# A two-layer conditioned residual kernel: transposed output with its column factor applied at eviction, three of eight weight products summed in PSUM, and unrolled loops

## The reference

```python
ae = layernorm(cond, g, b); h = gelu(ae @ w1 + b1); xw = h @ w2 + b2     # w2 is 512 x 8192
x_a, x_b = split(xw)                       # each [8, 512, 8]
layer = base_layer + x_a @ x_b^T           # per batch, 512 x 512
x = x + (x + x @ layer)                    # = x @ (2 I + layer)
ys = cond / sqrt(512)
d  = rsqrt((ys*ys) @ (W*W) + 1e-8)         # [8, 512], W = L1 weight
x = x + ((x * ys) @ W) * d                 # = x @ (I + diag(ys) W diag(d))
```

## Time and profile before

| | us |
|---|---|
| runs | 321.42, 321.53, 321.64 |
| span of the profiled execution | 319.6 |
| runs' median less that span | 1.93 |
| PE busy (share of the span) | 307.4 (96%) |
| DVE busy | 157.8 (49%) |
| ACT busy | 135.8 (42%) |
| POOL busy | 43.2 (14%) |

### The profile page before, as it was taken

One profiled execution on the slowest core, in us unless ns is written; L12 is line 12 of the kernel. 1 busy time (PEld: TensorE's weight loads), 2 busy tenths in 40 slices (PEclk: granted clock), 3 DMA queues, 4 the chain that ended last, 5 costly groups with the idle time before them and its releaser, 6 DMA issues.

```text
span 319.6 us, 4287 instructions
## 1 busy us (share of the span) xinstructions
PE 307.4 (96%) x1425; PEld 234.9 (74%) x1425; DVE 157.8 (49%) x230; ACT 135.8 (42%) x219; POOL 43.2 (14%) x59
## 2 busy tenths in 40 slices
PE   7979999999999958999999999999999999999995
PEld 7756555555566835888888888888888888888884
DVE  4898626262658896544255236146235434443300
ACT  3465233232366323546436337426435444454321
POOL 5545000000004991101001001001010000000000
PEclk9999999999999996999999999999999999999999
DMA  6921888788860130034375355437436545643342
GB/s 192 384 91 49 277 297 267 289 269 299 332 222 17 57 107 2 1 120 156 122 262 193 137 197 205 189 131 257 179 105 246 198 147 180 249 155 124 131 164 98
DMA packets 12892, 56.72 MB, mean 177 GB/s; under 512 B 2016, under 2 KB 2048, under 8 KB 8656
## 3 DMA queue, kind: packets, MB, share of 16 engines
q1 hardware_dynamic: 12880, 56.57, 49.4%
HBM read 39.77 MB, written 16.79 MB: 177 GB/s over the span
## 4 chain that ended last, share of the span: by engine, by line
PE 85%; DVE 7%; ACT 4%; issue 2%; DMA 1%; SPq 0%; DVEq 0%; ACTq 0%
PE tile L913 54%; PE tile L834 20%; PE acc L814 5%; PE aux L852 2%; DVE rtmp L601 1%; PE tile L770 1%; DMA base<-in_w0T 1%; DVE xs L615 1%; DVE base L521 1%; DVE rtmp L605 1%; ACT xs L351 1%; DVE xs L529 1%; DVE xs L526 1%; ACT rs L379 1%; PE aux L876 1%
## 5 line engine op out<-in xcount | busy, mean ns | idle before, releaser
L834 PE MATMUL tile<-rs,w0s 128*128 128x512 f32 x336 | 85.3, 406 | 5.3 <-ACT base L384 5.3
L913 PE MATMUL tile<-pev,xs 128*128 128x512 f32 x384 | 90.3, 389 | 0.0
L913 PE MATMUL tile<-w0s,xs 128*128 128x512 f32 x384 | 89.6, 389 | 0.0
L834 PEld LDWEIGHTS tile<-rs,w0s 128*128 128x128 f32 x336 | 63.0, 193 | 32.9 <-issue 14.4
L913 PEld LDWEIGHTS tile<-pev,xs 128*128 128x128 f32 x384 | 72.1, 188 | 15.0
L913 PEld LDWEIGHTS tile<-w0s,xs 128*128 128x128 f32 x384 | 72.1, 188 | 15.0
L456 ACT COPY stream<-tile 128x512 f32<-128x512 f32 x64 | 37.6, 587 | 99.9 <-PE tile L913 98.9
L615 DVE TENSOR_TENSOR xs<-xr,xs 128x1024 fp32r<-128x1024 f32 x32 | 40.5, 1267 | 62.5 <-ACT xs L414 62.5
L379 ACT CAST rs<-rtmp 128x512 fp32r<-128x512 f32 x28 | 17.4, 622 | 56.5 <-DVE rtmp L605 56.5
L697 DVE TENSOR_TENSOR base<-aux,base 128x512 f32 (+1 forms) x32 | 21.2, 686 | 34.7 <-PE aux L852 34.7
L414 ACT CAST xs<-xr 128x1024 fp32r<-128x1024 f32 x32 | 33.5, 1051 | 0.0
(11 more groups left out here) (112 smaller groups left out, 143.8 us busy)
## 6 DMA issues: line engine op xcount, KB each, us to landing
stream<-in_w2u SPq DMA_DIRECT2D x16, 1024.0 KB, 4.9
xr<-in_xT SPq DMA_DIRECT2D x32, 512.0 KB, 3.4
out<-stream SPq DMA_DIRECT2D x15, 1024.0 KB, 4.1
dbs<-d_kept SPq DMA_DIRECT2D x6, 256.0 KB, 4.5
base<-in_w0T SPq DMA_DIRECT2D x4, 256.0 KB, 4.7
w1s<-in_w1n SPq DMA_DIRECT2D x4, 256.0 KB, 5.0
base<-in_wm SPq DMA_DIRECT2D x1, 1024.0 KB, 7.2
stream<-in_w0n SPq DMA_DIRECT2D x1, 1024.0 KB, 6.6
```

The costliest lines, as they stand in the source:

```text
L834: last = nc.tensor.matmul(tiles[cc][:], w0s[:, u, kc, cols], rs[:, kc, v], start=kc == 0 and (u, v) == (0, 0), stop=kc == KC - 1 and (u, v ...
L913: mm = nc.tensor.matmul(tiles[tt][:], xs[:, h, u, cc, toks], p_split(parity)[:, v, cc], start=n == 0, stop=n == 11)
```

## The change

- The output is made transposed: P's columns are stationary and x moves, so a tile is 128 features x 512 tokens. The factor d is now one number per partition, and ScalarE applies it when it evicts the tile (`scale=dts[...]`). The host transposes the result.
- R becomes diag(ys) W + diag(1/d), so it needs no row of d: the diagonal takes `dinv` = d * (d2 + 1e-8), where d2 is the sum of squares. `dbs`, `dbc`, `d_kept` and all their transfers are gone. 1/d has to be there before the first base product, so batch 0 has no form of its own any more: `first_tiles`, GpSimd's repair of batch 0 and the second load of W0 are gone, and all eight batches go through `r_build`. 16 more warm-up matmuls stand before batch 0.
- Squares of W are made on ScalarE instead of GpSimd; W is loaded ahead of W0.
- Only batches 0 to 4 make their base products ahead and store them. Batches 5 to 7 make theirs in the main stage (`late_base`), in `aux0` and `aux1`, with the rank matmul summed into the same bank, and ScalarE and VectorE split straight from PSUM.
- The 16 units of w2 are spread over 11 groups of batches 0 to 2, by `W2_AFTER`.
- P's two parts have buffers of their own (`qs`). Stores are 512 KB each, in four slots, the last ones too. All loops are unrolled.

```diff
+W2_AFTER = {(0, 1): 1, (0, 2): 1, (0, 3): 1, (1, 0): 1, (1, 1): 1, (1, 2): 2, (1, 3): 2,
+            (2, 0): 2, (2, 1): 2, (2, 2): 2, (2, 3): 1}
...
+            def load_w2(unit):
+                if unit >= 2:
+                    sp.wait_ge(acc2_steps, 1 + unit - 1)
+                sp.dma_start(stream[:, unit % 2], w2u[unit]).then_inc(w2_loaded[unit % 2], 16)
...
             for kc in range(KC):
+                sp.dma_start(w1s[:, kc], w1n[:, kc]).then_inc(w1_loaded[kc], 16)
+            for kc in range(KC):
                 sp.dma_start(w0raw[:, kc], w0T[:, kc]).then_inc(w0_loaded[kc], 16)
-                sp.dma_start(w1s[:, kc], w1n[:, kc]).then_inc(w1_loaded[kc], 16)
...
+            for kc in range(KC):
                 act.wait_ge(w1_loaded[kc], 16)
+                nc.scalar.activation(w1sq[:, kc], w1s[:, kc], ACT.Square).then_inc(w1sq_ready, 1)
...
+            def r_scale(b, kc):
+                n = b * KC + kc
+                slot = rtmp[:, kc % RTMP]
+                if n >= RTMP:
+                    dve.wait_ge(r_lo, n + 1 - RTMP)
+                nc.vector.tensor_scalar(slot, w1s[:, kc], ys[:, b, kc:kc + 1], None, ALU.mult).then_inc(r_scaled, 1)
+                dve.wait_ge(r_scaled, n + 1)
+                blk = slot[:, kc * P:(kc + 1) * P]
+                nc.vector.scalar_tensor_tensor(blk, ident[:], dinv[:, b, kc:kc + 1], blk, ALU.mult,
+                                               ALU.add).then_inc(r_eyed, 1)
...
+                nc.scalar.activation(pairs[:, m % 4, o % 2], tiles[n % BANKS][:], ACT.Copy,
+                                     scale=dts[:, b, o:o + 1]).then_inc(bank_free, 1)
...
+            def late_base(b):
+                pe.wait_ge(r_lo, b * KC + KC)
+                for cc in range(KC):
+                    aux_free(b, cc)
+                    cols = slice(cc * P, (cc + 1) * P)
+                    for kc in range(KC):
+                        for u, v in ((0, 0), (0, 1), (1, 0)):
+                            last = nc.tensor.matmul(aux[cc % 2][:], w0s[:, u, kc, cols], rs[:, kc, v],
+                                                    start=kc == 0 and (u, v) == (0, 0), stop=False)
+                    if cc == KC - 1:
+                        last.then_inc(r_used, 3)
+                    rank_tile(b, cc, start=False)
...
+            def with_w2(b, kc):
+                if (b, kc) == (0, 0):
+                    pe.wait_ge(wm_loaded, 16)
+                    pe.wait_ge(ae_ready, 1)
+                    narrow(1, ae, wms).then_inc(h_done, 1)
+                    pe.wait_ge(b2_loaded, 16)
+                    pe.wait_ge(consts_ready, 4)
+                    nc.tensor.matmul(acc2[:], sel2[:], b2s, start=True, stop=True,
+                                     skip_group_check=True).then_inc(acc2_steps, 1)
+                    pe.wait_ge(h_copied, 1)
+                    nc.tensor.transpose(aux[0][:, 2 * P:3 * P], h_rows, ident[:]).then_inc(h_turned, 1)
+                for _ in range(W2_AFTER.get((b, kc), 0)):
+                    w2_unit()
...
+                        last.then_inc(tile_done, 1)
+                        if h == 0 and b + 1 < STORED:
+                            aux_free(b + 1, o)
+                            rank_tile(b + 1, o)
+                    if h == 0 and STORED <= b + 1 < B:
+                        late_base(b + 1)
```

More of the change, by code:

```diff
@@ L221, in _ @@
[L221 to L234, removed]
@@ L251, in _ @@
-            with sp.Fori(0, B - 1) as b:
-                for h in range(HALVES):
[L253 to L262, removed]
@@ L266, in _ @@
+            for i in range(4):
+                sp.wait_ge(stored[i], 16 * B)
         @block.gpsimd
@@ L375, in _ @@
-            nc.scalar.copy(d_rows, aux[1][0:B * KC, 2 * P:3 * P]).then_inc(d_copied, 1)
-            def r_high(b, kc):
-                act.wait_ge(r_eyed, b * KC + (kc + 1 - KC))
-                nc.scalar.copy(rs[:, kc, 0], rtmp[:, kc % RTMP]).then_inc(r_hi, 1)
-            def evacuate_base(b, chunks=range(KC)):
-                for cc in chunks:
-                    act.wait_ge(tile_done, b * KC + (cc + 1))
-                    nc.scalar.copy(base[:, b, cc, :], tiles[cc][:]).then_inc(bank_free, 1)
+            r_high(0, 2)
@@ L386, in _ @@
+            r_high(0, 3)
             act.wait_ge(z_ready, 1)
             nc.scalar.activation(lns[:, 15], lns[:, 11], ACT.Gelu).then_inc(h_ready, 1)
[L388 to L399 removed]
@@ L401, in _, with x_high, squared_rows @@
-            with act.Fori(1, LOOPED + 1) as b:
-                base_step(b)
+            for b in range(3):
+                base_step(b)
+            def x_high(b, h, cp):
+                act.wait_ge(x_loaded[cp], 16 * (b * HALVES + h + 1))
+                if b > 0:
+                    act.wait_ge(tile_done, main_tile(b - 1, h, KC - 1) + 1)
+                nc.scalar.copy(xs[:, h, 0, 2 * cp:2 * cp + 2, :], xr[:, cp]).then_inc(x_hi, 1)
+            def squared_rows(to, g, bank, n):
+                act.wait_ge(perm_done, n)
+                nc.scalar.copy(to[:, g], bank[:]).then_inc(squared, 1)
@@ L840, in base_tiles, with aux_free, rank_tile @@
                                 last.then_inc(r_used, 1)
-                    if units:
-                        w2_unit(b, kc)
-                    if between:
-                        between(b, kc)
-            def rank_tile(b, parity, cc, group, first=False):
+                    between(b, kc)
+            def aux_free(b, cc):
+                n = b * KC + cc
+                if n >= 2:
+                    pe.wait_ge(p_summed if n - 2 < EARLY else p_lo, n - 1)
+            def rank_tile(b, cc, start=True):
@@ L848, in rank_tile @@
                 pe.wait_ge(amk_ready, b + 1)
-                if not first or cc >= 2:
-                    pe.wait_ge(p_summed, b * KC + (cc - 1))
-                rows = csq[:, bass.ds(group, 1), :].rearrange("p o n -> p (o n)")
-                nc.tensor.matmul(aux[cc % 2][:], amk[:, parity, cc * P:(cc + 1) * P], rows, start=True,
+                nc.tensor.matmul(aux[cc % 2][:], amk[:, b % 2, cc * P:(cc + 1) * P], csq[:, b // 4], start=start,
                                  stop=True).then_inc(ac_done, 1)
+            def late_base(b):
+                pe.wait_ge(r_lo, b * KC + KC)
+                for cc in range(KC):
+                    aux_free(b, cc)
[7 more added lines that the diff above has]
+                    rank_tile(b, cc, start=False)
@@ L861, in columns_and_c @@
+            for b in range(3):
+                base_tiles(b, with_w2)
             def columns_and_c(b, kc):
@@ L901, in _ @@
-            base_tiles(7, between=first_rank_tiles)
-            def main_step(b, parity, group, last=False):
+                elif kc == 3:
+                    pe.wait_ge(c_lo, 1)
+                    pe.wait_ge(squared, 2)
+                    permute(acc2, 2, csp)
+                    permute(aux[0], 3, csp)
+            base_tiles(3, columns_and_c)
+            def first_rank_tiles(b, kc):
+                if kc in (1, 2):
+                    if kc == 1:
+                        pe.wait_ge(squared, 4)
+                    for cc in (2 * kc - 2, 2 * kc - 1):
+                        aux_free(0, cc)
+                        rank_tile(0, cc)
@@ L911, in main_step @@
                         for cc in range(KC):
                             for u, v in ((0, 0), (0, 1), (1, 0)):
-                                mm = nc.tensor.matmul(tiles[tt][:], xs[:, h, u, cc, toks],
-                                                      p_split(parity)[:, v, cc], start=n == 0, stop=n == 11)
-                                n += 1
-                        mm.then_inc(tile_done, 1)
-                        if h == 0 and not last:
-                            rank_tile(b + 1, 1 - parity, tt, group)
@@ L922, in _ @@
-            with pe.Fori(0, B // 2 - 1) as pair:
-                main_step(pair * 2, 0, pair // 2)
-                main_step(pair * 2 + 1, 1, (pair + 1) // 2)
-            main_step(B - 2, 0, 1)
-            main_step(B - 1, 1, None, last=True)
+                                last = nc.tensor.matmul(tiles[n % BANKS][:], qs[:, b % 2, u, cc, cols],
+                                                        xs[:, h, v, cc], start=cc == 0 and (u, v) == (0, 0),
+                                                        stop=cc == KC - 1 and (u, v) == (1, 0))
```

673 lines of the change are left out of this document (275 added, 398 removed).

## The result

The changed kernel takes 330.31 us (median of 4 runs, 329.0 to 331.55) against 321.58 of the kernel before: 1.026 times as long, 95% interval 1.023 to 1.030. The forecast was 324.0, in a range of 320.2 to 328.5. The direction was right; the loss was 8.7 us where 2.5 were forecast, three and a half times as much, and outside the range. The profiled execution is the longest of the four; its span is 329.5 against 322.05 in the sum.

A forecast was written before the change was run, and what follows sets the result against it. The prediction took the kernel as bound by TensorE work laid end to end, with about 8.5 us to win. Six terms plus 0.5 for late batches summed to a 322.05 us span; adding 1.93 gave 324.0, range 320.2 to 328.5.

The forecast's parts named there:

- (a): Opening, from the start to batch 0's second group, with d and `ae` needed first: 21.3 us, bounds 19.5 and 23.
- (b): TensorE's work from batch 0's second group to the first main tile, base groups, w2 units and small products: 75.2 us.
- (c): TensorE's waits for w2 loads, units 6, 8, 10, 12 and 14 each waiting 1.2: 6.5 us taken, 4 to 7.5.
- (d): Rank chain: no wait in the middle, but batch 0's own P comes late; wait 1.25 us (0.5 to 2.5).
- (e): Main stage: 180.5 us as before plus 12 late base groups at 2.72, and 0.5 for late batches' waits.
- (f): End after the last tile, eviction and one 512 KB store: 4.2 us against 3.57 before.
- 8.5 us of waiting and low clock in the middle: Loss in the kernel before, ahead of its first main tile: 6.6 us waiting, 1.9 lower clock, forecast as won.
- R3: Rival, main stage: late batches wait for R, costing 6.3 us instead of 0.5, total 329.8; chance 9%.
- the cheap scaling: Low-end price of `r_scale` on VectorE, about half of 0.73 us; a late batch's last `r_low` then ends at 9.9.
- R4: Rival: granted clock falls in a new wait, opening or w2, costing about 3.4 us, total 327.4; chance 8%.

The follow-up runs named there:

- Three slots: One more 1 MB slot for the w2 loads, three instead of two, all else as the changed kernel: 325.13 us.
- quiet GpSimd: Changed kernel with GpSimd's four W0 low-part subtractions cut to 8 of 512 columns, the rest set to zero: 324.08 us.
- the two with moved operations: Both with four w2 slots: R's two first scalings before the first add_two, 317.53 us; second narrow product and bias ahead of batch 0, 315.0 us.
- filled opening: Changed kernel plus ten warm-up matmuls between batch 0's first group and the second narrow product, also called clock kept up: 326.8 us.
- the last kernel: Four w2 slots, second narrow product and bias put ahead of batch 0, ten extra warm-ups out again: 315.0 us, 0.978 of the kernel before.

## Why the prediction was right or wrong

The sum against the profile, by its own terms, in us of span:

| term | forecast | measured | from |
|---|---|---|---|
| (a) to batch 0's second group | 21.3 | 24.8 | timeline, chain |
| slow matmuls in that group | 0 | 1.2 | 3.95 in the chain for 2.72 |
| (b) work to the first main tile | 75.2 | 75.1 | the remainder |
| (c) waits for w2 | 6.5 | 8.7 | gaps between units in the chain (8.2 in the view of waits) |
| slow matmuls after them | 0 | 1.7 | 1.48 and 4.13 for 0.99 and 2.95 |
| (d) first P | 1.25 | 0.8 | the wait on `qs` |
| (e) main stage with late groups | 213.6 | 213.4 | chain |
| (f) end | 4.2 | 3.9 | chain, page |

- (b), (d), (e) and (f) hold to half a microsecond, though (b) only as what the other rows leave. Durations of the chain before could be added up for another order of the same work. The 8.5 us of waiting and low clock in the middle were won as forecast (though TensorE idled only 5.3 of them, and the low clock slowed twelve matmuls and not eight: the four from 119.44 us took 2.05), and R3 (late batches that wait) did not come: in the first late batch the last `r_low` ends 0.8 us before TensorE turns to it, where the forecast gave a margin of 1.0 with the cheap scaling.
- (c) was right in mechanism, place and count. Units 6, 8, 10, 12 and 14 waited, as said. I walked to 6.0 and took 6.5; measured 8.7, since two of the five loads took longer than the 4.9 of the median (5.56 and 6.80 in the chain). Three slots suggest why: loads that overlap near the engines' full share take 6.5. In the windows of these two the share was 0.92 and 0.82, so for the longer one the cause stays open. The upper end given for it, 7.5, was too low.
- (a) failed in two parts. `ae` came at 20.3 instead of 18.7: GpSimd blocked VectorE four times (1.51, 1.26, 1.25 and 0.81 us operations), not one or two. The quiet GpSimd showed it: without the blocks `ae` came at 16.8, inside the 16.3 to 17.5 of the forecast. The new `r_scale` took 0.48 and 0.35 us. The Trainium skill (SBUF — State Buffer, "SBUF: two separate sides") has the two engines lock one port pair for a whole instruction, VectorE where its operation reads two SBUF inputs or runs in a two-port mode. The trace agrees: the four long ones are three operations with two tensors, down to one of 32 columns (1.25 us instead of 0.19), and the tensor_scalar, while a reciprocal beside the first subtraction took its usual 0.35. The price of a block was right (0.6 to 1.1) and the count was not: in this kernel and in the two with moved operations each of GpSimd's four subtractions made one operation long, so here the count was that of GpSimd's instructions.
- The step that failed most is R4, the clock. It stood at 8% and at nothing in the sum, with the argument that a wait of 1.2 us is far less than what came before the drop of the kernel before. In the sum, TensorE ran at the full level wherever it ran. The changed kernel's two drops came after single waits of 2.15 and 2.78 us, with shorter ones ahead of them. The clock accounts for 1.9 of the miss in (a), 1.2 behind it and 1.7 behind (c): 4.8 of the 7.5 us. The filled opening took 3.5 us off with nothing else changed. R4's price of 3.4 was near the 3.1 of the first stretch and twice the 1.7 of the second; a drop should have been part of the forecast, and twice.
- What makes a drop come is not settled. The length of the wait does not tell: 1.86 us (quiet GpSimd) and 1.93 (three slots) were followed by one, 2.69 (clock kept up) was not. Nor does the busy time in the 8 us rows of the profile: 4.72 and 5.74 were followed by one, 5.27 and 5.22 were not.
- The forecast's bookkeeping of gain and loss stands: what the change wins is the middle; what it gives back is the opening, which TensorE no longer fills, and the doubled units. The losses belong to two slots, one order of small products and the clock, and not to the transposed output or the late products; the last kernel keeps all of these and is faster than before.

Open are why the w2 waits bring a drop in some executions and not in others, and why one load took 6.8 us.

## What to carry to other kernels

When a change adds idle stretches to the bounding engine, price the clock with them: take the cost of a drop from the trace before as a term of the sum, with a chance, once for each new idle stretch. A wait shorter than the one before a known drop is no reason to leave it out. A double-buffered load is priced by the time between asking for it and needing it at its closest place, not by the average rate; more slots helped here until the DMA share was full. Work whose inputs come late leaves a hole at the front: put other ready work there, and if there is none, work that computes nothing.

## What the runs showed of the hardware

- A tensor_scalar of 128 x 512 float32 from SBUF took 0.48 us alone; the two-tensor operation that it replaced took 0.73.
- Even an operation of VectorE on 32 columns (0.19 us) took 1.25 beside a GpSimd subtraction, and the subtraction that met a 0.69 us operation of VectorE already under way took 1.77 instead of 1.27. When one operation was moved out of the way, the next ones took the blocks over (1.36, 1.38 us).
- Two units of w2 back to back take 1.85 us, two apart 0.99 each plus 0.23 for the change.
- One load of 1 MB lands 4.9 us after issue with at most two under way, 6.5 to 6.6 in the median with three or four slots, at 359 to 382 GB/s over windows of 10 us.
- The granted clock fell to the half level after single waits of TensorE of 1.86 to 3.92 us, and stayed up after one of 2.69.
